# Spreading the six merge pieces of a strip over four double steps as two, one, two, one

## What is computed

```
x = x + L0(gn(x))     gn: mean and variance over 32 groups of 6 channels
x = x + L1(gn(x))

L0(x): q, k, v = 1x1 convolutions of x; windows of 8 x 8 pixels, 6 heads of 32 channels
       o    = irfft2(rfft2(q) * rfft2(k)) in each window
       attn = softmax(o @ v^T + bias by relative position)
       y    = attn @ v, then a 1x1 convolution (proj)
L1(x): edges = 3x3 Laplacian of x, channel by channel
       y     = 1x1 convolution of (x + edges) (merge) + bias
```

## Time and profile before

| | us |
|---|---|
| median of 3 runs | 5898.05 |
| lowest and highest | 5894.93, 5898.69 |
| the profiled execution | 5900.44 |
| its span | 5898.6 |
| busy PE, PEld | 5629.3, 4715.9 |
| busy DVE | 4388.0 |
| busy ACT, POOL | 3320.2, 3326.2 |
| granted clock of PE, mean | 0.987 of full |

### The profile page before, as it was taken

The page is one execution under the profiler, slowest core; times in us unless marked ns, Lnnn a source line. Parts: engine busy times, 40 slices in busy tenths (PEclk is TensorE's granted clock), DMA queues, the critical chain, the costliest instruction groups (busy, mean ns, idle before and its releaser), DMA issues.

```text
span 5898.6 us, 207339 instructions
## 1 busy us (share of the span) xinstructions
PE 5629.3 (95%) x91644; PEld 4715.9 (80%) x91644; DVE 4388.0 (74%) x7534; ACT 3320.2 (56%) x6404; POOL 3326.2 (56%) x2342
## 2 busy tenths in 40 slices
PE   7999999999999999999999999999999999999977
PEld 5888788888888888887788878888888888888854
DVE  5777777787777777777777778777787787776754
ACT  3666655555555555555555655555555555555522
POOL 1333346665666655665566655665656666666643
PEclk9999999999999999999999999999999999999988
DMA  4222133323333233332333333333333322232245
GB/s 133 74 59 59 56 80 107 106 75 101 98 105 106 78 99 102 107 102 73 101 107 109 91 87 95 103 109 86 91 98 108 107 77 77 82 85 78 80 107 135
DMA packets 392497, 550.51 MB, mean 93 GB/s; under 512 B 24822, under 2 KB 284601, under 8 KB 391610
## 3 DMA queue, kind: packets, MB, share of 16 engines
q1 hardware_dynamic: 391612, 537.24, 32.3%
HBM read 335.82 MB, written 201.33 MB: 91 GB/s over the span
## 4 chain that ended last, share of the span: by engine, by line
PE 80%; ACT 9%; DVE 9%; issue 2%; POOL 0%; SPq 0%; DMA 0%; DVEq 0%; POOLq 0%; ACTq 0%
PE b_q L540 22%; PE b_t L638 7%; PE b_s L656 7%; PE b_q L624 7%; PE b_t L614 6%; PE b_s L488 4%; PE b_t L596 3%; PE b_s L490 3%; PE b_s L547 3%; PE b_s L550 3%; PE b_s L501 3%; ACT qkh L983 2%; PE b_s L499 2%; ACT probs L1056 2%; PE b_s L559 2%; ACT probsT L983 2%
## 5 line engine op out<-in xcount | busy, mean ns | idle before, releaser
L1133 POOL TENSOR_TENSOR probs<-probs,srec 128x768 f32<-128x768 f32 x512 | 881.7, 1722 | 1678.8 <-DVE srec L966 1678.8
L1120 POOL TENSOR_TENSOR probs<-probs,smax 128x768 f32<-128x768 f32 x512 | 755.0, 1475 | 603.9 <-DVE smax L926 603.4
L983 ACT ACTIVATE vs<-b_q 128x192 f32<-128x192 f32 x1024 | 339.7, 332 | 1282.2 <-PE b_q L540 1282.2
L915 DVE TENSOR_TENSOR qkl<-b_q,qkh 128x384 fp32r<-128x384 f32 x1024 | 570.2, 557 | 588.4 <-ACT qkh L983 556.3
L921 DVE TENSOR_TENSOR probs<-b_s,posb 128x768 f32<-128x768 f32 x512 | 490.3, 958 | 676.4 <-PE b_s L656 675.1
L540 PE MATMUL b_q<-wnh,xh 128*128 128x288 f32 x2048 | 703.6, 344 | 68.3 <-DVE qkl L915 65.6
L540 PE MATMUL b_q<-wnl,xh 128*128 128x288 f32 x2048 | 606.8, 296 | 0.0
L540 PE MATMUL b_q<-wnl,xhl 128*128 128x288 f32 x2048 | 605.8, 296 | 0.0
L540 PE MATMUL b_q<-wnh,xl 128*128 128x288 f32 x2048 | 605.7, 296 | 0.0
L540 PE MATMUL b_q<-wnh,xhb 128*128 128x288 f32 x2048 | 605.0, 295 | 0.0
L1095 POOL TENSOR_TENSOR dg<-late 128x645 f32<-128x645 f32 x352 | 563.0, 1599 | 64.3 <-DMA late<-x_dram 50.5
(11 more groups left out here) (159 smaller groups left out, 13871.1 us busy)
## 6 DMA issues: line engine op xcount, KB each, us to landing
ld<-in_x SPq DMA_DIRECT2D x192, 512.0 KB, 4.6
late<-x_dram SPq DMA_DIRECT2D x112, 640.0 KB, 5.1
xs<-in_x SPq DMA_DIRECT2D x128, 512.0 KB, 5.5
x_dram<-late SPq DMA_DIRECT2D x128, 512.0 KB, 2.9
out<-late SPq DMA_DIRECT2D x128, 512.0 KB, 2.9
late<-x_dram SPq DMA_DIRECT2D x240, 192.0 KB, 5.8
xs<-in_x SPq DMA_DIRECT2D x128, 256.0 KB, 5.7
x_dram<-late SPq DMA_DIRECT2D x128, 256.0 KB, 3.6
```

Of the source, the lines that this page charges most:

```text
L915: V.tensor_tensor(qkl[:, i % 2, :], q_out, qkh[:, i % 2, :].bitcast(F32), ALU.subtract).then_inc(lo_out, 1)
L983: return A.activation(o, i, ACT.Copy)
L1120: P.tensor_tensor(probs[:, i % 2, :, :], probs[:, i % 2, :, :], smax[:, i % 2, :].unsqueeze(2).broadcast_to([128, 12, N]), ALU.subtract).t ...
L1133: P.tensor_tensor(probs[:, i % 2, :, :], probs[:, i % 2, :, :], srec[:, i % 2, :].unsqueeze(2).broadcast_to([128, 12, N]), ALU.mult).then_ ...
```

## The change

The six pieces stand in slots 0, 1, 2, 4, 5 and 6 of a block instead of 0 to 5; slots 3 and 7 are free and take the small products (ph // 4 picks the first or second). All counts and waits that named the last piece's slot (5) name slot 6. In the part where the merge is alone, PE waits for the slot before the last only at slots 1, 2, 5 and 6, and for the last one at 0, 3, 4 and 7; a function act_reads says which slots ScalarE reads, still pieces 0 to 3.

```diff
 LOAD = 1024
 NLOAD = 3
 BIAS_ROWS = (64, 96)
-PIECES = 6
+PIECE_SLOTS = (0, 1, 2, 4, 5, 6)
+LAST_SLOT = PIECE_SLOTS[-1]
 HEADS = (0, 1, 4, 5, 2, 3)
 STENCIL_LAG, MERGE_LAG = 18, 19
 
...
         def m_task(it):
 
             blk, ph = divmod(it, 8)
-            if ph < PIECES:
+            if ph in PIECE_SLOTS:
                 v = blk - MERGE_LAG
-                return ("piece", v, ph) if 0 <= v < STRIPS else None
+                return ("piece", v, PIECE_SLOTS.index(ph)) if 0 <= v < STRIPS else None
             img, at_blk = divmod(blk, NS)
             if at_blk == 1 and 1 <= img <= B:
-                return (("mean", "dev")[ph - 6], img - 1, 0)
-            if at_blk == 2 and ph == 6 and 1 <= img <= B:
+                return (("mean", "dev")[ph // 4], img - 1, 0)
+            if at_blk == 2 and ph == 3 and 1 <= img <= B:
                 return ("mbias", img - 1, 0)
             if at_blk == 12 and 0 <= img < B - 1:
-                return (("gmean", "gspread")[ph - 6], img + 1, 0)
+                return (("gmean", "gspread")[ph // 4], img + 1, 0)
             if at_blk == 14 and 0 <= img < B - 1:
-                return ("bias", img + 1, ph - 6)
+                return ("bias", img + 1, ph // 4)
             return None
+
+        def act_reads(it):
+
+            task = m_task(it)
+            return task is not None and it >= ALONE and task[0] == "piece" and task[2] < 4
 
         iterations = range(-4, 8 * BLOCKS)
         ALONE = PAIRS + 2 * 8
         m_count, d_count, a_count = {-5: 4}, {-5: 4}, {-5: 0}
         for it in iterations:
-            by_act = it >= ALONE and it % 8 < 4
             m_count[it] = m_count[it - 1] + (m_task(it) is not None)
-            d_count[it] = d_count[it - 1] + (m_task(it) is not None and not by_act)
-            a_count[it] = a_count[it - 1] + (m_task(it) is not None and by_act)
+            d_count[it] = d_count[it - 1] + (m_task(it) is not None and not act_reads(it))
+            a_count[it] = a_count[it - 1] + act_reads(it)
 
         border_count = list(itertools.accumulate(int(v % NS < 3 or v % NS == NS - 1) for v in range(STRIPS)))
 
...
             def source_load(v):
                 b, s = divmod(v, NS)
                 if v >= 3:
-                    m_wait(sp, 8 * (v - 3 + MERGE_LAG) + PIECES - 1)
+                    m_wait(sp, 8 * (v - 3 + MERGE_LAG) + LAST_SLOT)
                 for n in (v, v + 1) if s + 1 < NS else (v,):
                     sp.wait_ge(x1_sent[n % 2], 32 * (n // 2 + 1))
                 for tensor, part, chan, first, count in (
...
 
             def result_store(v):
                 b, s = divmod(v, NS)
-                m_wait(sp, 8 * (v + MERGE_LAG) + PIECES - 1)
+                m_wait(sp, 8 * (v + MERGE_LAG) + LAST_SLOT)
                 for o, part, chan, first, count in (
                         (res_a, slice(0, CA), slice(0, CA), s * WS, 8),
                         (res_b, slice(0, CB), slice(CA, C), s * WS, 4),
...
                 if not task:
                     return
                 kind, at, p = task
-                m_wait(pe, it - 2 if it > ALONE else it - 1)
+                m_wait(pe, it - 2 if it > ALONE and it % 4 in (1, 2) else it - 1)
                 if pair(2):
                     pe.wait_ge(s_out, pair(2)[1])
                 if kind == "piece":
...
                 if not task:
                     return
                 kind, at, p = task
-                if kind == "piece" and it >= ALONE and p < 4:
+                if act_reads(it):
                     return
                 dve.wait_ge(m_mm, m_count[it])
                 if kind == "piece":
...
 
             def a_result(it):
                 task = m_task(it)
-                if it >= ALONE and task and task[0] == "piece" and task[2] < 4:
+                if act_reads(it):
                     _, v, p = task
                     if p == 0:
                         act.wait_ge(out_sent[v % 2], 48 * (v // 2))
...
                 if unit == 0:
                     act.wait_ge(src_in[v % 3], 48 * (v // 3 + 1))
                     if v >= 2:
-                        act.wait_ge(m_mm, m_count[8 * (v - 2 + MERGE_LAG) + PIECES - 1])
+                        act.wait_ge(m_mm, m_count[8 * (v - 2 + MERGE_LAG) + LAST_SLOT])
                 A.activation(zz, src[:, r + 1:r + 5, 1:W + 1], ACT.Copy, scale=5.0).then_inc(five_done, 1)
 
             for j, pair in doubles():
```

## The result

The kernel became slower, which the forecast held for the less likely side. 5995.66 us median (5989.21 to 6005.69, 4 runs) against 5898.37 us of the kernel before beside it (4 runs): ratio 1.0169, 95% interval 1.0154 to 1.0183. The forecast was 5894 us, the range 5873 to 5914; the time lies 82 us above its upper end. The profiled execution's span is 6003.8 us against 5898.6, 105.2 us more.

The account below looks back on a forecast made before the run. PE is busy 95% of the span, yet waits on DVE's remainder and ScalarE's probsT copy where no piece covers them. Terms -33 + 21 + 8 + 0 + 3 - 3 = -4 us gave 5894 us, range 5873 to 5914.

Parts of the forecast that it names:

- all four rivals: Cheap means 5871 us (0.27), tail eats the gain 5910 to 5931 (0.14), locked copy 5908 (0.08), no ordinary gain 5927 (0.07).
- Ordinary blocks: 79 blocks without small products or scaling: moved pieces shorten double steps 1 and 2, lengthen 3; -0.42 us each, -33 us.
- Mean and group mean: 2nd and 13th block, double step 1: DVE chain waits for GpSimd, scores late; +1.7 us, twice per image, +21 us.
- the clock's part: Behind PE's 2.7 us gap before the moved means' scores, 1.2 GHz for a while: 1.3 us every second time, +8 us.
- the locked copy: Means' last copy on DVE also locked out by GpSimd's next subtraction: 1.18 us more in 12 places, 5908 us; chance 0.08.
- the cheap means: DVE gets in between GpSimd's operations, one 1.5 us wait gone in 12 places, clock stays up: 5871 us; chance 0.27.
- The other small products: Bias part 0, merge bias and 14th block (missing piece gains nothing, double step 3 pays 0.60): 0, bounds -5 and +6.
- Startup: Before the strips start (blocks 12 to 18), mean and group mean stand once each without cover: +3 us.
- The tail: From block 130: piece 3 waits for ScalarE's read, +0.74; L852 -0.61; shorter PE gap; 17 strips -3 us, bounds +13, -15.
- the tail that eats the gain: Blocks 130 to 146: piece 3's full 0.74 us wait stays, 5910 us, or 5931 with more clock falls; chance 0.14.
- ordinary blocks without gain: A GpSimd or ScalarE wait stands where the piece was, so ordinary blocks gain nothing: 5927 us; chance 0.07.

Follow-up runs that it names:

- gate: Changed kernel with SP's release of the source load put back to its earlier place in time; 5909.19 us median, 1.002 of the kernel before.
- split: Changed kernel with the first statistics load held back until slot 4, early burst 1.0 MB instead of 1.5; 5932.55 us, ratio 1.006.
- light: Changed kernel with merge source loads cut to a quarter of their rows from strip 3 on, SP's waits unchanged; 5915.98 us, ratio 1.0035.
- early: Kernel before, pieces unmoved, with only SP's release of the source load one slot earlier (slot 2); 5960.02 us, ratio 1.0103.
- release2: gate with PE released once the mean's and group mean's products are read, not at chain end; second batch, 5881.47 us, ratio 0.9976.
- relold: Kernel before with only the early release of the mean's and group mean's region; 5897.3 us, ratio 1.0002.

## Why the prediction was wrong

**The step that failed** is one that the sum does not have. The prediction went through what each engine computes and what each wait on m_read costs, and looked for queued work behind the waits that the change adds. It never asked what an empty slot 3 does to the waits that were there: SP's release of the source load counts products, and with no product in slot 3 its count is reached one slot earlier, 5 us in time. No term, no bound and no rival had it; all four rivals lie on DVE, ScalarE, GpSimd and PE. It is worth 86 us of the 97 (gate). The loss then comes by a path that the prediction did not look at either: the source load and statistics load run while PE uses up its program fastest, and its next instructions come late. In the profile of the changed kernel the ordinary blocks are +64 us where -33 was forecast; all else together is +41 where +29 was. The share of the DMA engines, 0.33 over the long stretch, gave no warning, since it is a mean over bursts that fill them.

**Ordinary blocks: right.** Medians of the four double steps in the changed kernel are 10.68, 10.00, 11.03 and 10.34 us, 42.05 in all, where 10.7, 10.0, 11.0, 10.35 and 42.05 were forecast. Block 72:

```profile
3243.66 0.93 PE L661 MATMUL b_s<-vT,osb 32*64 32x64 f32 x48
3249.02 0.41 PE L591 MATMUL b_t<-ident_sb,vs 128*128 128x128 f32 x2
3251.21 0.77 PE L619 MATMUL b_t<-probsT,vs 64*32 64x64 f32 x48
3253.65 0.93 PE L661 MATMUL b_s<-vT,osb 32*64 32x64 f32 x48
```

L591 to L619 takes 2.19 us where a piece had made it 2.86. With the stops the mean block of this kind is 43.41 us long instead of 42.60 before; in gate it is 42.14. All ordinary blocks together: -36 us in gate against the forecast -33, and +64 us in the changed kernel.

**Mean and group mean: the mechanism right, the clock's part too small.** Double step 1 of the 2nd and 13th block takes 12.80 and 13.04 us on average in the changed kernel, forecast near 12.7. The chain on DVE next to GpSimd in block 65 (double step 1 starts at 2932.93):

```profile
2941.00 1.97 POOL L1138 TENSOR_TENSOR probs<-probs,srec 128x768 f32<-128x768 f32 x1 [1.94 <-DVE srec L971]
...
2941.87 1.12 DVE L829 TENSOR_TENSOR sm<-sm 128x2 f32<-128x2 f32 x1
...
2942.94 1.54 POOL L1100 TENSOR_TENSOR dg<-late 128x645 f32<-128x645 f32 x1
...
2943.03 1.47 DVE L830 TENSOR_TENSOR sm<-sm 128x2 f32<-128x2 f32 x1
...
2944.42 0.16 DVE L831 COPY sm<-sm 128x2 f32<-128x2 f32 x1
...
2944.72 0.93 PE L661 MATMUL b_s<-vT,osb 32*64 32x64 f32 x48 [1.79 <-DVE sm L831]
```

L829 ends with L1138 (2942.99 and 2942.97), L830 with L1100 (2944.50 and 2944.48), and the scores start 11.79 us in, forecast 11.8. The last copy took 0.16 us, begun just before L1100's end, and was through as L1110 began: the rival of the locked copy has fallen here, and so has that of the cheap means. The Trainium skill, SBUF — State Buffer, Who interferes with whom, says that a vector instruction with two SBUF inputs contends with a GpSimd instruction that reads SBUF, and calls the shared ports an exclusive lock; for L829 and L830, with two SBUF operands, the trace agrees (1.12 and 1.47 us for 2 elements), while an SBUF to SBUF copy in the midst of GpSimd's operation stands in no row read. The two kinds of block together are +31 us in the changed kernel, +35 in split, +38 in light and +45 in gate, where 21 and 8 were forecast. What varies is the clock: half clock in these blocks is 3 us before, and 31, 38, 44 and 61 us in the four. From the first to the last that is 13.4 us for 30.6 us more of it, 0.44 us each. So my estimate for the part without the clock is 31.4 - 0.44 x 31 = 18 us (forecast 21), and for the clock's part 14 to 27 us (forecast 8). That the clock falls behind every second of these waits was right for the changed kernel (6 of 12), but in gate it was 10 of 12, and what I left out is the half clock elsewhere in these blocks. Double step 1 itself has about its forecast size in gate (13.00 and 13.13 instead of 10.7). The rest there is mostly in double step 2 of the 13th block, 12.58 us instead of 11.38 where a gain of 0.35 was forecast, and in double step 0 of the 2nd block, 15.12 instead of 13.97. The latter stands ahead of the mean and takes 14.87 us in early, where no mean was moved, so it is not shown to be a price of the change. In release2 half clock there is 7 us and the two kinds cost +8.3 us. Not all of the double step behind is the clock: release2 still has 12.35 us there, without half clock. In its block 60 gmean's chain on DVE ends only 1.5 us into double step 2, and the subtraction behind it (L925) starts 3.2 us in, where L915 had ended 2.64 us in the earlier trace rows.

**The other small products: too small as well.** The 14th block was put at nothing; over its six occurrences it is +11.0 us in gate and +9.2 in the changed kernel, outside the bounds of -5 and +6. Its double step 1 is shorter there (12.66 us on average instead of 14.56), which I had excluded, and double step 2 longer (17.49 instead of 14.63). The vector engine's casts hold PE either way; PE only reaches them earlier. Block 61, the piece behind them, before and after:

```profile
2715.80 0.65 PE L499 MATMUL b_s<-late,mn 128*64 128x256 f32 x4 [2.50 <-DVE probs L921]
```

```profile
2760.71 1.19 PE L493 MATMUL b_s<-late,mn 128*128 128x256 f32 x2 [3.96 <-DVE probs L926]
```

The idle time is 3.96 us instead of 2.50, and behind it the two passes take 1.19 us, those of half clock. From the start of the piece to the end of the scores it is 12.36 us instead of 9.93. The gap was moved, and grew into one after which the clock is low. In gate the 15th block gained 1.3 us and the 3rd 1.0, over six each.

**Startup**: blocks 0 to 18 take 2.7 us longer, forecast 3. That says little: they take 0.3 us longer in gate, and 1.6 in relold and 3.6 in early, where no piece was moved. **The tail**: 264.2 us behind the last scores instead of 265.3, forecast -3; the kernels with the old order of pieces have 261 to 265 us there (relold, early, before), those with the new one 263 to 267 (and light 273), so no gain is shown. Both steps of it are there:

```profile
5891.70 0.47 ACT L1011 ACTIVATE late<-b_s,mc 128x256 f32<-128x256 f32 x1 [0.30 <-PE b_s L497]
5892.31 0.67 PE L493 MATMUL b_s<-late,mn 128*128 128x256 f32 x2 [0.66 <-ACT late L1011]
...
5896.71 0.82 DVE L857 TENSOR_TENSOR probs<-late 128x645 f32<-128x645 f32 x1
5899.13 0.67 PE L493 MATMUL b_s<-late,mn 128*128 128x256 f32 x2 [2.86 <-DVE late L862]
```

Piece 3 waits 0.66 us for ScalarE's read of piece 2, L857 takes 0.82 instead of 1.44, and PE's long gap is 2.86 us, forecast 2.87. A cycle at full clock is 11.6 us instead of 11.32 (forecast +0.13), but the others are mostly 13.28 where they were 13.0 or 13.8. The shorter gap did not keep the clock up more often. The rival of the tail that eats the gain has fallen, and that of ordinary blocks without gain.

**The sum again.** The changed kernel's profile against that of the kernel before: ordinary blocks +64.4, 2nd and 13th +31.4, 14th +9.2, 3rd and 15th -1.4, startup +2.7, tail -1.1 = +105.2 us. For gate against the kernel before, both profiled: ordinary blocks -36.5, 2nd and 13th +44.8, 14th +11.0, 3rd and 15th -2.3, startup +0.3, tail +2.0 = +19.3 us, and the spans differ by 19.4. Forecast had been -4. This profile of gate is of an execution 10.7 us slower than the median of its eleven (granted clock 0.982, their median 0.985); by medians gate is 9.8 us above the kernel before, so the terms with the clock in them are at their high end here. With SP's release left where it was in time the change comes out at 1.002: inside the range, and slower than the forecast by the clock and the 14th block.

**Where the half clock is.** In the long stretch it is 167 us in the changed kernel, 126 in gate and 48 before. By kind of block, in that order: ordinary 75, 0, 0; 14th 44, 51, 31; 2nd and 13th 31, 61, 3; 3rd 17, 14, 14. The 75 us are 16 stretches, and each begins within a stop of 2.07 us or more, or up to 1.6 us behind it. It does not take so long a stop: in early six stretches in ordinary blocks begin at or behind stops of 1.4 to 1.9 us.

What stays open: why the clock falls at some gaps of the same length and not at others (6 of 12 places in the changed kernel, 10 of 12 in gate), why q8's packet comes after the data of a burst and not between them, and how many packets PE can have ahead. That PE had used up its instructions rests on the place of the stops and on the time from packet to restart; the profile has no record of what PE's buffer holds.

## What to carry to other kernels

When a step is moved out of a place, list every wait of every engine that counts it, and ask for each when the count is now reached; a wait that is met earlier costs nothing on its own engine and can start a transfer in a worse place. For a DMA burst the question is not only who needs its data, but what PE does while it runs: keep it off stretches of many small matmuls with a weight load each. In a trace, a wait on "issue" in the midst of equal matmuls, at a whole number of instruction packets, is the sign of it. And release a PSUM region with the operation that reads it, not at the end of the chain behind it: worth 25 us where PE stands behind, nothing where it doesn't.

## What the runs showed of the hardware

PE can stop for want of its own instructions in straight-line code. Here its program comes in 16 KB packets over a DMA queue that shares the 16 engines with the data: 26 stops of 1.8 us on average in double step 1 when 1.5 MB of loads begin 13 us into a block, 24 of 0.8 us with 1.0 MB, 2 of 0.5 us with 0.8 MB, and none when the same 1.5 MB begin 5 us later, over fewer and longer matmuls. One packet stands for 256 of PE's records, all 86 stops of the four kernels in double steps 1 and 2 lie at the same remainder of 256, and PE goes on 1.20 to 1.62 us after the packet's end. The Trainium skill, Runtime: NRT & Kernel Launch, Instruction fetch mechanics, says that the sequencer fills its instruction memory in blocks of 16 KiB by its own DMA queue, which the packets of q8 agree with, and that the fetch is hidden because instructions are issued slower than they are filled in. The row of 48.1 us of "issue" and the stop behind the 33rd of 48 products speak against that second part, for a kernel that fills the DMA engines at the same time.

The lock between DVE and GpSimd held in each row read: 2-element operations with two SBUF operands took 1.12 and 1.47 us and ended with GpSimd's operation, while L832, a copy of 4 elements from PSUM, took 0.16 us in the midst of L1143. In the changed kernel's trace the mean and group mean have 26 such 2-element operations beside GpSimd (L829, L830, L707, L708): 14 took 1.12 to 1.13 us, 12 took 1.47 to 1.49, and all ended within 0.03 us of GpSimd's operation. The six with no operation of GpSimd beside them took 0.16.
